# Full values kept in place in PSUM, and residual sums moved to GpSimd, in a chain of four conditioned blocks

## The chip, the cores and the metric

One core of a Trainium2 chip runs the whole program. The metric is device microseconds of that core, from one launch; the text below calls them us. The core has TensorE (PE: its matmuls; PEld: its weight loads), VectorE (DVE), ScalarE (ACT), GpSimd (POOL) and the queue of SyncE (SP), which only issues DMAs. GpSimd doesn't read or write PSUM in this kernel.

## The reference, cut to what matters

An input x of 16 batches, 256 rows of 256 float32 each, goes through four blocks. Each block has two parts, and each part is "normalise, modulate, transform, gate, add to x":

```python
norm = _ln(x) * (1.0 + scale[:, None]) + shift[:, None]      # scale, shift, gate: from a small vector per batch
h = gelu(norm @ w1 + b1)                                      # or an attention in its place
x = x + gate[:, None] * (h @ w2 + b2)
```

The eight parts are the stages 0 to 7 of the kernel. Stages 0, 1, 3, 4, 5 and 7 are two-layer networks with hidden widths of 256, 512, 1024, 512, 512 and 1024. Stage 2 is an attention with 16 heads of 64, stage 6 one with a single head of 256. In stage 4 the sum is kept only where a mask of rows says so (`where(m, fwd + bwd, 0)`), and the other rows of x stay as they are. In stage 7 a second gelu stands between h @ w2 + b2 and the gate.

## The kernel before, in words

**Numbers in two pieces.** Every matmul of values is made of three (`split3`, lines 255 to 257): a float32 value is kept as a rounded "hi" piece and a "lo" piece, lo being the full value minus hi. So each operand costs three steps outside TensorE: an activation that writes the full value, an activation that writes hi (both on ScalarE, from the same PSUM bank), and a subtraction on VectorE that writes lo. In the networks the full hidden value goes to an SBUF buffer `hf` (line 571), and VectorE subtracts `hf - hh` into `hl` (line 577). In the normalisation the full value goes to `nf` (line 392) and the subtraction is line 399.

**Stages and groups.** A network stage works on groups of two batches (512 columns), 8 groups a stage. The hidden layer is cut into chunks of 128: 2, 4, 8, 4, 4 and 8 chunks in stages 0, 1, 3, 4, 5 and 7. `ff_body` writes one group's program for each engine. For chunk c, TensorE first computes the hidden chunk c+2 (`ff_hidden`; it belongs to the next group when c+2 runs over), then the output of chunk c (`ff_output`). Two PSUM banks (`U_BANKS`) take the hidden chunks in turn, and two pairs of banks (`Y_BANKS`) take the outputs of even and odd groups.

**Order on each engine.** Each engine runs its own list in order, and semaphores tie the lists together. VectorE's list in a group of stage 1, 3, 4, 5 or 7: at c = 0 take the previous group's output (`ff_take`, line 608: output times gate into `upd`, two batches), the lo of unit 0 (`ln_rest`, line 399), the lo of a hidden chunk; at c = 1 the lo of unit 1, the statistics of the group after next (`ln_stats`, lines 320 to 330), the lo of a chunk; at c = 2 the lo of a chunk, the normalisation `xn` (`ln_norm`, line 342), the rounding of the next stage's weights (`weights_hi`, line 293), and the residual sum x = upd + xb of the previous group's first batch (`ff_add`, line 641); at c = 3 the lo of a chunk and the second batch's sum. In stage 4 the sum is a series: copy x, copy the mask's words, add, two predicated copies, copy back (lines 626 to 639). In stage 7 it is line 618.
GpSimd's list in a group: 1/sqrt (`ln_rsqrt`, line 334, one small power instruction for each of the two units), the lo of the next stage's weights (`weights_lo`, line 300), then xb = x + gated bias for this group's two batches (line 802), which waits until x of the group before is new. In stage 7 the third step is the gating after the second gelu (`ff_gate2`, line 652).
SyncE loads weight slices (when `weights_lo` of the last slice is done) and the gate rows of each batch, and in stage 7 stores x.

**Attention.** In stage 2 TensorE goes through 16 heads a batch. GpSimd divides the probabilities (line 1023), VectorE does the residual once a batch (`res_vector`, lines 1096 and 1101). Stage 6 has one turn a batch (`sh_turn`): VectorE's list is statistics of batch b+3, scaling of the probabilities, residual of b-1, lo pieces, `ln_norm` of b+3, the row maxima, the lo of the unit b+2 and the weights. One buffer `agate` holds the gate of a batch, and its load waits until the batch before has been added.

**PSUM banks of the transposes.** `ln_transpose` (line 379) writes a unit into bank 7 or 6 (in stage 0 always bank 7, in stage 2 bank 1), and the next unit for a bank waits for `ln_nf`, ScalarE's last read. Between stages that aren't chained (1 to 2, 2 to 3, 5 to 6, 6 to 7) all engines meet at a barrier (`end_phase`).

Of the kernel before, what the change touches and what calls it, by code (L numbers as in the profile page):

```python
# [31 lines left out]
GB = 2  # L32
# [11 lines left out]
def bass_cond_blocks(nc, t, out):  # L44
# [62 lines left out]
    with ctx:  # L107
# [14 lines left out]
        mcur = sb("mcur", [P, GB, TPB], I32)  # L122

        stats = [sb(f"stats{j}", [P, TPB, 6]) for j in range(GB)]
        meanvar = [sb(f"meanvar{j}", [P, TPB, 2]) for j in range(GB)]
        vareps = [sb(f"vareps{j}", [P, TPB]) for j in range(GB)]
        rstd = [sb(f"rstd{j}", [P, TPB]) for j in range(GB)]
        mhalf = sb("mhalf", [P, TPB])
        xn = [sb(f"xn{j}", [P, ROWW]) for j in range(GB)]
        nf = [sb(f"nf{j}", [P, ROWW]) for j in range(GB)]  # L130
# [14 lines left out]
        hf = [sb(f"hf{i}", [P, GW], scope=ffn) for i in range(HRING)]  # L145
# [19 lines left out]
        agate = sb("agate", [P, 2 * D], scope=att)  # L165
# [69 lines left out]
        aupd_ready = sem("aupd_ready"); ax_new = sem("ax_new"); agate_loaded = sem("agate_loaded")  # L235
# [74 lines left out]
        def ln_stats(dve, p, b, j):  # L310
            u = p * BATCH + b
            if p and early(b, 2 * GB + 2):
# [5 lines left out]
                dve.memset(spacer[:, 1:2], 0.0)  # L318
# [17 lines left out]
        def ln_norm(dve, p, b, j):  # L336
            u = p * BATCH + b
            dve.wait_ge(ln_rstd, u + 1)
            if not early(u, sets(p, b)):
                dve.wait_ge(ln_tp, u + 1 - sets(p, b))  # L340
            for k in range(TPB):
                last = dve.tensor_scalar(xn[j][:, k * D:(k + 1) * D], x[:, bass.ds(b * ROWW + k * D, D)],  # L342
                                         meanvar[j][:, k, 0:1], rstd[j][:, k:k + 1], ALU.subtract, ALU.mult)
            last.then_inc(ln_xn, 1)

        def head_norms(name, eng, p):

            for n in heads(p):
                if name == "gpsimd":
                    ln_rsqrt(eng, *n)  # L350
                else:
                    ln_stats(eng, *n)
# [1261 lines left out]
```

## Time and profile before

| what | value |
|---|---|
| median of 3 runs | 1899.54 us (1896.93 to 1900.22) |
| the profiled execution's own time | 1899.73 us |
| its span, first to last instruction | 1897.6 us |
| busy: PE | 1754.8 us, 92% of the span |
| busy: VectorE | 1355.4 us, 71% |
| busy: ScalarE | 1146.9 us, 60% |
| busy: GpSimd | 873.6 us, 46% |
| mean granted TensorE clock | 0.966 |

The stages follow each other in the trace: stage 0 up to about 130 us, stage 1 to 250, stage 2 to 1121, stage 3 to 1330, stage 4 to 1455, stage 5 to 1537, stage 6 to 1697, stage 7 to the end. A busy share is an average over stages with different limits, so the table says little by itself: what a change is worth in a stage is read from that stage's own windows and waits.

### The profile page before, as it was taken

To read this page: it belongs to the slowest core of one execution; us is meant where nothing else is said; L and a number is where in the kernel's file an instruction comes from. 1 tells how busy PE (TensorE), PEld (TensorE's weight loads), DVE (VectorE), ACT (ScalarE), POOL (GpSimd) and SP (SyncE) were. 2 spreads that over 40 slices of the span, in tenths; PEclk is the share of its full clock that TensorE was granted. 3 is DMA by queue.
4 is the path that set the end of the run, shared out by engine and by line. 5 is a ranking of instruction groups with operands and counts; after the bars stand their busy time and mean duration, and the time that the engine had idled before them with its cause. 6 is when DMAs were issued, how large, how long until landed. Compare 5 with 4: busy or idle time off the path is not lost.

```text
span 1897.6 us, 36653 instructions
## 1 busy us (share of the span) xinstructions
PE 1754.8 (92%) x12739; PEld 1587.3 (84%) x12739; DVE 1355.4 (71%) x3357; ACT 1146.9 (60%) x2858; POOL 873.6 (46%) x949
## 2 busy tenths in 40 slices
PE   5888979999999999999999979999888989989998
PEld 3657878888889888888889979999777978879997
DVE  5878866676777767677677665555999969985663
ACT  3445646666666666666666655556655746656664
POOL 1535645655665555656565533332444523331111
PEclk7999989999999999999999989999999989989999
DMA  8222200000000000000000001110111112220111
GB/s 288 64 56 70 87 20 4 10 10 10 10 10 10 9 8 10 4 10 10 10 10 10 7 15 31 29 30 27 47 43 50 52 25 44 46 58 23 45 45 45
DMA packets 110969, 65.87 MB, mean 35 GB/s; under 512 B 81530, under 2 KB 92788, under 8 KB 110788
## 3 DMA queue, kind: packets, MB, share of 16 engines
q1 hardware_dynamic: 110788, 63.54, 12.3%
q8 instruction: 104, 1.70, 0.4%
q14 instruction: 77, 0.63, 0.1%
HBM read 59.06 MB, written 4.46 MB: 33 GB/s over the span
## 4 chain that ended last, share of the span: by engine, by line
PE 77%; DVE 10%; issue 6%; ACT 5%; POOL 1%; DMA 1%; DVEq 0%; POOLq 0%; SPq 0%; ACTq 0%
PE bank L255 21%; PE bank L257 20%; PE bank L256 20%; PE bank L1036 7%; PE bank L985 6%; PE bank L379 2%; DVE xn L342 2%; DVE hl L577 1%; PE bank L438 1%; ACT nf L392 1%; DVE nTlo L399 1%; DVE aTlo L399 1%; ACT nThi L392 1%; ACT prob L1008 1%; DVE upd L608 1%
## 5 line engine op out<-in xcount | busy, mean ns | idle before, releaser
L1023 POOL TENSOR_SCALAR prob<-prob,rinv 128x256 f32<-128x256 f32 x512 | 467.3, 925 | 343.0 <-DVE rinv L1017 342.1
L571 ACT ACTIVATE hf<-bank,vecs 128x512 f32<-128x512 f32 x240 | 168.0, 700 | 302.4 <-PE bank L257 302.4
L577 DVE TENSOR_TENSOR hl<-hf,hh 128x512 fp32r<-128x512 f32 x240 | 196.7, 820 | 157.4 <-ACT hh L571 157.0
L1045 ACT ACTIVATE pthi<-bank 128x512 fp32r<-128x512 f32 x272 | 164.6, 605 | 196.5 <-PE bank L1036 193.9
L1008 ACT ACTIVATE prob<-bank,nmax 128x256 f32<-128x256 f32 x544 | 253.8, 479 | 39.6 <-DVE nmax L1281 21.1
L998 DVE TENSOR_REDUCE nmax<-bank 128x2 f32<-128x512 f32 x256 | 175.6, 686 | 142.1 <-PE bank L985 141.8
L334 POOL TENSOR_TENSOR rstd<-vareps,mhalf 128x2 f32<-128x2 f32 x128 | 106.1, 829 | 343.9 <-DVE vareps L330 343.2
L257 PE MATMUL bank<-WBhi,hh 128*128 128x256 f32 x768 | 217.7, 284 | 0.0
L256 PE MATMUL bank<-WBlo,hh 128*128 128x256 f32 x768 | 217.6, 283 | 0.0
L255 PE MATMUL bank<-WBhi,hl 128*128 128x256 f32 x768 | 217.3, 283 | 0.0
L255 PE MATMUL bank<-aThi,WAlo 128*128 128x256 f32 x576 | 177.4, 308 | 41.1 <-DVE aTlo L399 31.7
L1049 DVE TENSOR_TENSOR ptlo<-bank,pthi 128x512 fp32r<-128x512 f32 x272 | 186.2, 684 | 4.5 <-ACT pthi L1045 4.5
L255 PE MATMUL bank<-nThi,WBlo 128*128 128x512 f32 x384 | 158.0, 411 | 24.5 <-DVE nTlo L399 14.1
L392 ACT ACTIVATE nf<-bank,mod 128x256 f32<-128x256 f32 x256 | 148.1, 579 | 49.2 <-issue 28.3
L1036 PE MATMUL bank<-ident,prob 128*128 128x128 f32 x1088 | 172.6, 281 | 2.2 <-DVE prob L1291 2.0
L571 ACT ACTIVATE hh<-bank,vecs 128x512 fp32r<-128x512 f32 x240 | 167.3, 697 | 0.0
L257 PE MATMUL bank<-aThi,WAhi 128*128 128x256 f32 x576 | 166.1, 288 | 0.0
L256 PE MATMUL bank<-aTlo,WAhi 128*128 128x256 f32 x576 | 165.7, 288 | 0.0
L255 PE MATMUL bank<-pthi,vlo 128*128 128x256 f32 x512 | 148.8, 291 | 7.4 <-DVE oTlo L1078 7.4
L255 PEld LDWEIGHTS bank<-WBhi,hl 128*128 128x128 f32 x768 | 147.3, 192 | 8.1
L256 PE MATMUL bank<-nTlo,WBhi 128*128 128x512 f32 x384 | 153.6, 400 | 0.0
L256 PEld LDWEIGHTS bank<-WBlo,hh 128*128 128x128 f32 x768 | 147.1, 192 | 7.6
(164 smaller groups left out, 5310.6 us busy)
## 6 DMA issues: line engine op xcount, KB each, us to landing
gates<-gate_scratch SPq DMA_DIRECT2D x96, 256.0 KB, 3.7
agate<-gate_scratch SPq DMA_DIRECT2D x32, 256.0 KB, 3.2
stage<-in_L_cond_W SPq DMA_DIRECT2D x64, 64.0 KB, 2.3
out<-x SPq DMA_DIRECT2D x16, 256.0 KB, 2.2
adaw<-in_L_cond_Wc SPq DMA_DIRECT2D x1, 3072.0 KB, 17.9
stage<-in_L_cond_W_qkv SPq DMA_DIRECT2D x8, 384.0 KB, 3.5
x<-in_x SPq DMA_DIRECT2D x1, 2560.0 KB, 16.8
stage<-in_L_cond_ff_w SPq DMA_DIRECT2D x32, 64.0 KB, 2.1
```

Of the source, the lines that this page charges most:

```text
L255: pe.matmul(dst, lhs[1], rhs[0], start=start, stop=False, skip_group_check=True)
L256: pe.matmul(dst, lhs[0], rhs[1], start=False, stop=False, skip_group_check=True)
L257: return pe.matmul(dst, lhs[0], rhs[0], start=False, stop=stop, skip_group_check=True)
L392: last = act.activation(dst, T[:, c * SEQ:(c + 1) * SEQ], ACT.Identity, scale=mod[:, p, 0, c, bass.ds(b, 1)], bias=mod[:, p, 1, c, bass.ds ...
L571: last = act.activation(dst[:, :], U_BANKS[c % 2][:, :], ACTF[p], bias=vecs[:, at:at + 1])
L577: dve.tensor_tensor(hl[r][:, :], hf[r][:, :], hh[r][:, :].bitcast(F32), ALU.subtract).then_inc(h_lo, 1)
L998: dve.tensor_reduce(nmax[i][:, :], src.rearrange("p (q k) -> p q k", q=TPB), AX_X, ALU.max, negate=True).then_inc(nmax_ready, 1)
L1008: last = act.activation(dst[:, q, :], src[:, q * SEQ:(q + 1) * SEQ], ACT.Exp, scale=scale, bias=nmax[i][:, q:q + 1], accum_out=rsum[i][:, ...
L1023: last = pool.tensor_scalar(dst[:, q, :], dst[:, q, :], rinv[i][:, q:q + 1], None, ALU.mult)
L1036: last = pe.transpose(PTB[i][:, c * SEQ + q * P:c * SEQ + (q + 1) * P], src[:, q, c * P:(c + 1) * P], ident[:, :])
L1045: act.activation(pt[i][0][:, :], PTB[i][:, :], ACT.Copy).then_inc(pt_hi, 1)
L1049: dve.tensor_tensor(pt[i][1][:, :], PTB[i][:, :], pt[i][0][:, :].bitcast(F32), ALU.subtract).then_inc(pt_lo, 1)
```

## The change

Five edits, made together.

1. **Full values in place.** ScalarE writes hi first and then the full value over its own input in the PSUM bank. `hf` and `nf` are gone; the subtractions of lines 577 and 399 read the bank. The bank stays taken until the subtraction is done, so there are 4 U banks in place of 2 (TensorE waits for `h_lo` of four chunks back), and one pair of Y banks in place of two (the first output chunk of a group waits, bank by bank, for `y_taken` of the group before). The transposes wait for `ln_lo` in place of `ln_nf`.
2. **Residual sums on GpSimd.** `ff_add` and the new `res_add` run there. In stage 4 GpSimd adds into `act2`, and VectorE is left with two predicated copies a batch, straight into x (`ff_where`). In a group of GpSimd's list the previous group's sums (in stage 7 with the gating ahead of them) now stand first, before 1/sqrt.
3. **1/sqrt.** The addition of eps moves from VectorE to GpSimd, and the two units of a group share one addition and one power instruction.
4. **Stage 6.** `ln_norm` runs on GpSimd. Two gate buffers in place of one.
5. One-element memsets on VectorE are dropped.

```diff
@@ ln_stats, ln_rsqrt @@
-            dve.wait_ge(ln_mv, u + 1)
-            dve.tensor_scalar(vareps[j][:, :], meanvar[j][:, :, 1], EPS[p], None, ALU.add).then_inc(ln_ve, 1)
-        def ln_rsqrt(pool, p, b, j):
-            pool.wait_ge(ln_ve, p * BATCH + b + 1)
-            pool.tensor_tensor(rstd[j][:, :], vareps[j][:, :], mhalf[:, :], ALU.pow).then_inc(ln_rstd, 1)
+        def ln_rsqrt(pool, p, b, j, n=1):
+            u = p * BATCH + b
+            pool.wait_ge(ln_mv, u + n)
+            pool.tensor_scalar(vareps[:, j:j + n, :], meanvar[:, j:j + n, :, 1], EPS[p], None, ALU.add).then_inc(ln_ve, n)
+            pool.wait_ge(ln_ve, u + n)
+            pool.tensor_tensor(rstd[:, j:j + n, :], vareps[:, j:j + n, :], mhalf[:, j:j + n, :], ALU.pow).then_inc(ln_rstd, n)
+        def pool_norms(pool, units):
+            if units:
+                ln_rsqrt(pool, *units[0], len(units))
@@ ln_transpose, ln_modulate, ln_rest @@
-                pe.wait_ge(ln_nf, u if p == 0 or p == 1 and early(b, 2 * GB + 1) else u + 1 - sets(p, b))
+                pe.wait_ge(ln_lo, u if p == 0 or p == 1 and early(b, 2 * GB + 1) else u + 1 - sets(p, b))
-                for dst in (nf[j][:, c * SEQ:(c + 1) * SEQ], hi[c]):
+                for dst in (hi[c], T[:, c * SEQ:(c + 1) * SEQ]):
-            dve.tensor_tensor(lo, nf[j][:, :].rearrange("p (c r) -> p c r", c=DC), hi.bitcast(F32),
+            dve.tensor_tensor(lo, t_bank(p, b, j)[:, :].rearrange("p (c r) -> p c r", c=DC), hi.bitcast(F32),
@@ the networks @@
-        U_BANKS, Y_BANKS = bank[0:2], [bank[2:4], bank[4:6]]
+        U_BANKS, Y_BANKS = bank[0:HRING], bank[4:6]
-            if not early(n, 2):
-                pe.wait_ge(h_act, n - 1)
+            if not early(n, HRING):
+                pe.wait_ge(h_lo, n + 1 - HRING)
-            for dst in (hf[r], hh[r]):
-                last = act.activation(dst[:, :], U_BANKS[c % 2][:, :], ACTF[p], bias=vecs[:, at:at + 1])
+            for dst in (hh[r], U_BANKS[r]):
+                last = act.activation(dst[:, :], U_BANKS[r][:, :], ACTF[p], bias=vecs[:, at:at + 1])
-            dve.tensor_tensor(hl[r][:, :], hf[r][:, :], hh[r][:, :].bitcast(F32), ALU.subtract).then_inc(h_lo, 1)
+            dve.tensor_tensor(hl[r][:, :], U_BANKS[r][:, :], hh[r][:, :].bitcast(F32), ALU.subtract).then_inc(h_lo, 1)
-            if c == 0 and not early(GROUP_BASE[p] + g, 2):
-                pe.wait_ge(y_taken, GB * (GROUP_BASE[p] + g - 1))
+                if c == 0 and r % TPB == 0 and not early(GROUP_BASE[p] + g, 1):
+                    pe.wait_ge(y_taken, GB * (GROUP_BASE[p] + g - 1) + r // TPB + 1)
+        def ff_where(dve, p, g, batches=range(GB)):
+            for j in batches:
+                b = GB * g + j
+                dve.wait_ge(x_tmp, b + 1)
+                for k in range(TPB):
+                    last = dve.copy_predicated(x[:, b * ROWW + k * D:b * ROWW + (k + 1) * D],
+                                               maski[:, b * TPB + k:b * TPB + k + 1].to_broadcast([P, D]),
+                                               act2[:, j, k * D:(k + 1) * D])
+                last.then_inc(x_new, 1)
@@ ff_body, gpsimd @@
-                    for n in norms:
-                        ln_rsqrt(eng, *n)
+                    if prev and p == L3_FF:
+                        ff_gate2(eng, p, g - 1, 1 - i)
+                    if prev:
+                        ff_add(eng, *prev[:2])
+                    pool_norms(eng, norms)
...
+                    if left == 0 and not goes_on:
+                        ff_add(eng, p, g)
@@ the attentions @@
-            dve.wait_ge(axb_ready, n + 1)
-            dve.tensor_tensor(xs(b), aupd[:, :], axb[:, :], ALU.add).then_inc(ax_new, 1)
+        def res_add(pool, b, n):
+            pool.wait_ge(axb_ready, n + 1)
+            pool.wait_ge(ay_taken, n + 1)
+            pool.tensor_tensor(xs(b), aupd[:, :], axb[:, :], ALU.add).then_inc(ax_new, 1)
@@ mh_gpsimd: in the slot of head 4 @@
+                if i == 4 and not first:
+                    res_add(pool, b - 1, b - 1)
@@ sh_turn, gpsimd @@
                     ln_rsqrt(eng, *sh_batch(b + 3), n)
+                    ln_norm(eng, *sh_batch(b + 3), n)
+                if not first:
+                    res_add(eng, b - 1, BATCH + b - 1)
                 res_gpsimd(eng, b, BATCH + b)
```

## Rows read from the trace of the kernel before

**Rows 1.** Windows by stage: length, busy PE, PEld, DVE, ACT, POOL (us), clock, DMA, GB/s

```profile
130.00:250.00 120.00, 106.44 (x660) 95.56 (x660) 104.01 (x223) 67.40 (x124) 71.61 (x49) 0.95 0.27 76
...
255.00:1100.00 845.00, 808.70 (x6739) 751.65 (x6738) 587.58 (x1358) 548.08 (x1705) 505.36 (x570) 0.98 0.04 8
...
1332.00:1455.00 123.00, 103.92 (x640) 93.68 (x640) 117.29 (x362) 70.16 (x129) 50.19 (x49) 0.96 0.16 43
...
1465.00:1525.00 60.00, 60.00 (x395) 54.83 (x394) 51.80 (x129) 41.35 (x78) 31.37 (x34) 1.00 0.19 52
...
1555.00:1690.00 135.00, 126.46 (x996) 119.13 (x995) 128.01 (x333) 88.23 (x220) 40.85 (x57) 1.00 0.20 42
...
1700.00:1890.00 190.00, 188.75 (x1208) 171.39 (x1208) 104.62 (x224) 114.28 (x199) 31.45 (x29) 0.99 0.13 42
```

**Rows 2.** Line 608 in four stretches: count, min/median/max ns, first to last start

```profile
L608 DVE TENSOR_TENSOR upd<-bank,gates x15: 680/684/693, 1344.0 to 1450.8; 128x512 f32<-128x512 f32 x15
...
L608 DVE TENSOR_TENSOR upd<-bank,gates x12: 680/686/693, 1464.2 to 1525.4; 128x512 f32<-128x512 f32 x12
...
L608 DVE TENSOR_TENSOR upd<-bank,gates x16: 680/684/695, 143.3 to 239.6; 128x512 f32<-128x512 f32 x16
...
L608 DVE TENSOR_TENSOR upd<-bank,gates x14: 679/682/684, 1729.6 to 1870.8; 128x512 f32<-128x512 f32 x14
```

**Rows 3.** Who waited for line 399 in stage 4 (1332 to 1455 us): us, times

```profile
  PE bank L255: 17.8, 8
```

**Rows 4.** Groups of DVE in stage 4: count, busy us, mean ns, idle before

```profile
L577 DVE TENSOR_TENSOR hl<-hf,hh 128x512 fp32r<-128x512 f32 x33 | 31.3, 948 | 2.2 <-ACT hh L571 2.0
...
L633 DVE COPY_PREDICATED act<-mcur,upd 128x256 f32<-128x256 int32 x32 | 13.5, 476 | 0.7
...
L342 DVE TENSOR_SCALAR xn<-x,meanvar,rstd 128x256 f32<-128x256 f32 x32 | 11.0, 409 | 0.0
...
L629 DVE TENSOR_TENSOR upd<-upd,xb 128x512 f32<-128x512 f32 x16 | 10.9, 683 | 0.0
...
L627 DVE COPY act<-x 128x512 f32<-128x512 f32 x16 | 6.8, 423 | 0.0
```

**Rows 5.** The instructions that write xb, whole run: count, min/median/max ns

```profile
L802 POOL TENSOR_TENSOR xb<-x,gates x80: 1253/1301/1799, 51.9 to 1534.8; 128x512 f32<-128x512 f32 x80
```

**Rows 6.** Groups of POOL in stage 1 (130 to 250 us)

```profile
L802 POOL TENSOR_TENSOR xb<-x,gates 128x512 f32<-128x512 f32 x20 | 30.0, 1518 | 9.8 <-DVE x L641 9.8
...
L300 POOL TENSOR_TENSOR WAlo<-stage,WAhi 128x768 fp32r<-128x768 f32 x8 | 21.0, 2628 | 22.5 <-DVE WAhi L293 22.5
...
L334 POOL TENSOR_TENSOR rstd<-vareps,mhalf 128x2 f32<-128x2 f32 x13 | 11.7, 898 | 14.0 <-DVE vareps L330 13.7
...
L300 POOL TENSOR_TENSOR WAlo<-stage,WAhi 128x256 fp32r<-128x256 f32 x8 | 9.5, 1192 | 0.0
```

**Rows 7.** Who waited for line 399 in stage 6 (1555 to 1690 us)

```profile
  PEld bank L255: 11.3, 13
```

**Rows 8.** Timeline of DVE in one turn of stage 6: start, us

```profile
1614.58 1.71 DVE L342 TENSOR_SCALAR xn<-x,meanvar,rstd 128x256 f32<-128x256 f32 x2
```

**Rows 9.** A group of POOL in stage 6

```profile
L334 POOL TENSOR_TENSOR rstd<-vareps,mhalf 128x2 f32<-128x2 f32 x14 | 9.8, 700 | 3.8 <-DVE vareps L330 3.8
```

**Rows 10.** The page's costliest group (GpSimd in stage 2)

```profile
L1023 POOL TENSOR_SCALAR prob<-prob,rinv 128x256 f32<-128x256 f32 x512 | 467.3, 925 | 343.0 <-DVE rinv L1017 342.1
```

**Rows 11.** Who waited for line 399 in stage 2 (270 to 1098 us)

```profile
  PE bank L255: 27.7, 15
```

**Rows 12.** Timeline of ACT in one group of stage 7: start, us, idle before

```profile
1782.38 1.22 ACT L646 ACTIVATE act<-upd 128x512 f32<-128x512 f32 x2
...
1792.35 0.69 ACT L571 ACTIVATE hf<-bank,vecs 128x512 f32<-128x512 f32 x1 [1.55 <-PE bank L257]
```

**Rows 13.** Timeline of DVE at the very end

```profile
1892.27 2.34 DVE L618 TENSOR_TENSOR x<-x,act 128x512 f32<-128x512 f32 x2 [1.50 <-POOL act L652]
```

**Rows 14.** Timeline of PE at the start of stage 0

```profile
23.27 1.09 PE L379 MATMUL bank<-ident,xn 128*128 128x128 f32 x4 [2.18 <-ACT nThi L392]
```

More of the change, by code:

```diff
@@ L121, in bass_cond_blocks @@
         spacer = sb("spacer", [P, 8])
-        mcur = sb("mcur", [P, GB, TPB], I32)
         stats = [sb(f"stats{j}", [P, TPB, 6]) for j in range(GB)]
[L125 to L128, printed above, removed]
+        meanvar = sb("meanvar", [P, GB, TPB, 2])
+        vareps = sb("vareps", [P, GB, TPB])
+        rstd = sb("rstd", [P, GB, TPB])
+        mhalf = sb("mhalf", [P, GB, TPB])
         xn = [sb(f"xn{j}", [P, ROWW]) for j in range(GB)]
-        nf = [sb(f"nf{j}", [P, ROWW]) for j in range(GB)]
         pro = ExitStack()
@@ L164, in bass_cond_blocks @@
         aupd = sb("aupd", [P, ROWW], scope=att)
-        agate = sb("agate", [P, 2 * D], scope=att)
+        agate = [sb(f"agate{i}", [P, 2 * D], scope=att) for i in range(2)]
         smax = [sb(f"smax{i}", [P, TPB], scope=att) for i in range(2)]
@@ L311, in ln_stats @@
             u = p * BATCH + b
-            if p and early(b, 2 * GB + 2):
+            if p:
                 if p - 1 in HID:
@@ L344, in ln_norm @@
             last.then_inc(ln_xn, 1)
         def head_norms(name, eng, p):
-            for n in heads(p):
-                if name == "gpsimd":
-                    ln_rsqrt(eng, *n)
-                else:
-                    ln_stats(eng, *n)
+            if name == "gpsimd":
+                pool_norms(eng, heads(p))
             if name == "vector":
                 for n in heads(p):
+                    ln_stats(eng, *n)
+                for n in heads(p):
                     ln_norm(eng, *n)
+        def pool_norms(pool, units):
+            if units:
+                ln_rsqrt(pool, *units[0], len(units))
@@ L607, in ff_take, with ff_add @@
                 half = 1 if p == L3_FF else 0
-                dve.tensor_tensor(rows_of(upd[:, j, :]), rows_of(Y_BANKS[i][j][:, :]), gate_row(i, j, half),
+                dve.tensor_tensor(rows_of(upd[:, j, :]), rows_of(Y_BANKS[j][:, :]), gate_row(i, j, half),
                                   ALU.add if half else ALU.mult).then_inc(y_taken, 1)
-        def ff_add(dve, p, g, i, batches=range(GB)):
-            for j in batches:
+        def ff_add(pool, p, g):
+            for j in range(GB):
                 n = GB * (GROUP_BASE[p] + g) + j
@@ L845, in ff_norms @@
             if name == "gpsimd":
-                for n in ns:
-                    ln_rsqrt(eng, *n)
+                pool_norms(eng, ns)
         def ff_start(name, eng, p):
@@ L1224, in mh_gpsimd @@
                     head_norms("gpsimd", pool, A + 1)
+            if last:
+                res_add(pool, b, b)
         def mh_sync(sp, b, first, last):
```

93 lines of the change are left out of this document (33 added, 60 removed).

## The prediction, made before the changed kernel was run

> **What bounds the kernel now.** I read the windows by stage first. TensorE is busy 60.00 of 60 us in stage 5, 188.75 of 190 in stage 7 and 808.7 of 845 in stage 2; in stage 4 it is busy 103.9 of 123 while VectorE is busy 117.3, in stage 6 126.5 of 135 against VectorE's 128.0, in stage 1 106.4 of 120 against 104.0 [rows 1]. So two thirds of the time are TensorE's own, and an edit on the other engines can only lose there; stages 1, 4 and 6 are where VectorE's list sets the pace. The start times of the take (line 608) give periods: in stage 4 the groups follow each other in (1450.8 - 1344.0) / 7 = 15.26 us; in stage 5, with the same 4 chunks and the same matmuls, in (1525.4 - 0.6 - 1464.2) / 5 = 12.12 us, 0.6 being the step to the second batch; in stage 1, 4 chunks again, in (239.6 - 0.6 - 143.3) / 7 = 13.67 us [rows 2]. 12.12 is thus the floor of a four-chunk group. With 8 chunks, in stage 7, it is (1870.8 - 0.6 - 1729.6) / 6 = 23.43, so a chunk costs 2.83 and the eight transposes of a group 0.8. The waits agree: TensorE stands 17.8 us before line 399's lo pieces in stage 4 [rows 3].
>
> **Stage 4.** Off VectorE go, per batch, the add (0.683), the copy of x (0.423) and the copy back of the same shape (0.423): 1.53 x 16 = 24.5 us [rows 4]. What stays is the predicated copies. VectorE's busy time becomes 117.3 - 24.5 = 92.8 in 8.06 groups, 11.5 us a group, under the floor; eps, memsets and mask copies come off besides. The next thing that can be late is the single Y pair. The first output chunk of a group needs its bank taken. On VectorE the take stands behind the lo of a hidden chunk (0.68, as the add) and two predicated copies (2 x 0.48) [rows 4], about 1.6 us, then takes 0.68 itself [rows 2]: 2.3 us. TensorE has the eight transposes and one hidden chunk to do first, half of 2.83 since a chunk's columns are half hidden, half output: 0.8 + 1.4 = 2.2. The two are level; I add 0.45 a group for semaphores and order. So 12.6 in place of 15.26, and 12.2 for the first group of stage 5: 8 x 2.66 = 21 us. Bounds: 0 (another engine takes over at 15.26) to 25 (floor 12.12).
>
> Line 577 takes 0.948 on average here [rows 4], while line 608, of the same size but with a PSUM operand, takes 0.684 and never over 0.695 [rows 2]. The change makes line 577 such an instruction.
> The Trainium skill (SBUF — State Buffer, "Who interferes with whom") says that a VectorE instruction with two SBUF inputs contends with a GpSimd instruction that reads SBUF, and that one with at most one SBUF input doesn't. By that rule VectorE's load in stage 4 falls by another 33 x 0.26 = 8.7 us and GpSimd's adds run at their minimum; without it the durations of the rows before hold. The sum for stage 4 is the same either way, since both lie under the floor; stages 1 and 7 hang on it, through GpSimd.
>
> **Stage 1.** Its period should go from 13.67 to the floor, except where a weight slice's DMA holds VectorE's list in the first groups: I leave 3 us for that. 7 x (13.67 - 12.3) - 3 = 6.6; I take 7 us. GpSimd has to keep up, and it is in a loop with VectorE: sums of the last group, eps and power, (VectorE: normalise, round weights), lo of the weights, xb, and again. At the xb row's minimum of 1.25 [rows 5] sums and xb are 5.0, the weights 2.63 + 1.19, eps and power 1.0, VectorE's part 4 x 0.34 + 0.7: 11.9 us, just under 12.12. At the means of this stage (1.518 for sums and xb, two powers 1.8) it is 6.1 + 3.8 + 1.8 + 2.1 = 13.8 [rows 6]. I take the lower end, since fewer of VectorE's instructions meet GpSimd's. Bounds: +1 to -11 us.
>
> **Stage 6.** TensorE's weight loads stand 11.3 us in 13 turns before line 399, 0.87 a turn [rows 7]. Just ahead of it VectorE spends 1.71 on the two instructions of the normalisation [rows 8], which move to GpSimd, and 0.68 on an add as in [rows 4], which moves too. That is more than 0.87, so the wait should go: -11 us. On GpSimd the normalisation costs 2 x 0.925 by the weighing row, of the same shape with one operation in place of two [rows 10]; with power 0.70 [rows 9], eps 0.3, sum and axb 2 x 1.3 [rows 5], weights at most 1.2 [rows 6]: 6.7 us of a turn that is now 135 / 14 = 9.6, 14 being the powers there [rows 9]. Were the two-operation form twice as slow, 8.5, about the new turn of 8.7. The wait for the gate's DMA goes off GpSimd's list with the second buffer. At the stage's start one normalisation sits on the path: +1.4. Bounds: -12 to +3.
>
> **Stages 2, 3, 5.** In stage 2 TensorE waits 27.7 us, 15 times, behind transposes, four activations and line 399 [rows 11]. The chain keeps its links and their lengths: 0. GpSimd's new sum (1.3) stands in one slot of 16; it idles 343 us over 256 heads, 1.34 a slot [rows 10], so it is hidden; without that cover it would cost 1.3 x 15 = 20. Stages 3 and 5 are at the floor and stay.
>
> **Stage 7.** 1/sqrt now stands behind two gatings and two sums. The second gelus run from 1782.38 [rows 12]; the first is done at about 1783.1; four GpSimd instructions of 1.3 end at 1788.3; eps and power (0.3 + 1.1, the power on four elements estimated between 0.70 and 1.8) 1789.7; normalising 1.4, line 577 0.7: 1791.8. TensorE wants that lo when the hidden chunk whose activation starts at 1792.35 is done [rows 12]. Slack 0.5 us: I take 0, bound +8 (1.6 x 5 groups with the means above).
>
> **The ends.** At each barrier after a network, sums of 1.25 in place of 0.68 for the last two batches: +0.8, twice; after the attentions +0.6, twice. At the very end the sums stand behind both gatings: VectorE's pair starts at 1892.27, when the first gating is done, and ends at 1894.6 [rows 13]; GpSimd's second gating ends 1.25 later, at 1893.5, and two sums after it at 1896.0: +1.4. Together +4.2. At the start of stage 0 the transposes of a unit wait for the lo, not for the activation alone (TensorE stood 2.18 there [rows 14]): +0.7 twice, and the joined 1/sqrt +1.2 twice: +3.8; VectorE's lighter list returns about as much in the rest of the stage: 0, bounds -4 to +4.
>
> **The sum.** -21 - 7 - 11 + 1.4 + 4.2 = -33.4 us. The profiled execution's own time is 1899.7 (its span 1897.6), the median of the runs 1899.5, so the two scales agree: 1866.3; I say 1866.
>
> **What ScalarE's writes cost.** No row shows an activation that writes PSUM. From both sides: as now (0.69, or 1.22 for two in a row [rows 12]), or twice that for the half that is written in place. ScalarE idles 1.55 of a 2.8 us chunk in stage 7 [rows 12], but in stage 5 it is busy 41.4 of 60 and would be at 62 [rows 1]. I take "as now".
> The Trainium skill (ScalarE: Activation LUTs, "Step-by-step: what each stage is for") says that ScalarE writes PSUM faster than SBUF. By it stage 2's chain would shorten and the sum be a few us lower; no row here bears on it.
>
> **The rivals.**
> A, the forecast: 1866, chance 0.60, its own range 1855 to 1878.
> B, GpSimd becomes the bound: stage 1 at 13.8 (0 gained), stage 7 +8, stage 6 half gained. For it: the loop of 11.9 us is 0.2 under the floor. Against: GpSimd is busy only 71.6 of 120 in stage 1. -21 - 5.5 + 8 + 4.6 = -14: 1886. Chance 0.18.
> The Trainium skill (GPSIMD Engine Reference, "4.1 Engine selection") advises VectorE for elementwise work on tiles, GpSimd being about 2 times slower with two inputs. The trace agrees: 1.25 against 0.68.
> C, more than forecast: stage 4 at 12.12, stage 1 without its DMA wait, stage 0 gains 4, stage 2's chain shorter by 0.3 x 15: 1866 - 4 - 3 - 4 - 4 = 1851. Chance 0.10.
> D, slower: a bank-writing activation takes twice as long. ScalarE is then the bound of every four-chunk group: in stage 4 (70.2 x 1.5) / 8.06 = 13.1 us. Stage 4 gains 8 x 2.2 = 17, stage 1 gains 4, stage 5 loses 1 x 7, stage 2's chain is 0.9 longer 15 times, 13.5, stage 6 gains nothing, and ends and starts cost 9.4 (stage 0 without its return): +9, 1909. It decides from an extra of about 0.8 of an activation's time; at 0.5 the kernel is still faster. Against: line 608 reads PSUM at no extra cost. Chance 0.07.
> E, the edits don't do what they say, or gains and ends cancel: within 4 us of before. Chance 0.05.
>
> **Range and chances.** 1849 to 1889 holds A, B and most of C. What a measurement of this kernel tells from no change is about 0.2%, 3.8 us. Faster 0.88, same 0.05, slower 0.07.
>
> **What would show it.** Periods of line 608: 12.6 in stage 4 (15.26: something else binds; over 13: ScalarE, or the take), 12.3 in stage 1's later groups (13.8: B). Line 577 at 0.69 everywhere. No wait of TensorE before line 399 in stage 6, and 1.85 as before, 15 times, in stage 2. GpSimd's power on four elements near 1.1. In stage 7, TensorE's wait on line 577 none. The in-place activations at 0.69. The forecast is wrong if stage 4's period doesn't fall, or if TensorE's busy share in stages 2, 3, 5 or 7 does.

## The result, and the profile after

The changed kernel takes 1876.47 us (median, 1872.67 to 1880.09) beside 1899.88 for the kernel before on the same chip: a ratio of 0.9872, 95% interval 0.9851 to 0.9894. The forecast was 1866 with a range of 1849 to 1889. The direction and the range hold; of the 33 us forecast 23 came. The profiled execution took 1872.67 us, span 1870.9; it is the fastest of the four, so the two traces differ by 26.8 us where the medians differ by 23.4. One execution of the kernel with values through SBUF, further down, ran at a mean granted clock of 0.65 (2422.96 us, the others 1872 to 1878) and is left out of that kernel's times.

Where these microseconds came from is read from the starts of the takes (line 609 now), which mark every group. The sizes are differences of such starts in the two traces, and the changes are rounded last:

| stretch | before | after | change | forecast |
|---|---|---|---|---|
| start to the first take | 54.9 | 58.7 | +3.8 | +3.8 |
| rest of stage 0 | 78.8 | 75.1 | -3.7 | -3.8 |
| stage 1 (133.7 to 248.3; 133.8 to 249.2) | 114.6 | 115.5 | **+0.9** | **-7** |
| stage 2, with its ends | 901.6 | 902.1 | +0.5 | +1.4 |
| stage 3 | 179.9 | 178.6 | -1.3 | 0 |
| stage 4, to the second take of 5 | 134.3 | 115.3 | -19.1 | -21 |
| stage 5 | 71.1 | 73.2 | +2.0 | 0 |
| stage 6, with its ends | 194.3 | 183.3 | -11.0 | -8.2 (-11 + 1.4 + 0.8 + 0.6) |
| stage 7 | 159.8 | 160.2 | +0.3 | 0 |
| end | 8.1 | 9.0 | +0.8 | +1.4 |

The windows by stage answer to [rows 1] (length, busy PE, PEld, DVE, ACT, POOL, clock, DMA, GB/s):

```profile
130.00:250.00 120.00, 107.63 (x660) 96.44 (x660) 75.66 (x175) 66.68 (x124) 76.49 (x70) 0.93 0.27 76
1332.00:1455.00 123.00, 119.86 (x765) 106.99 (x764) 92.90 (x247) 81.14 (x150) 70.52 (x79) 0.99 0.20 53
1555.00:1690.00 135.00, 128.28 (x997) 122.56 (x996) 103.07 (x277) 94.73 (x226) 98.90 (x115) 0.99 0.23 50
```

In the window of stage 4 TensorE is busy 119.9 of 123 us where it was 103.9; the changed kernel leaves stage 4 at 1432.2, so 23 us of this window are stage 5, and from 1342.4 to 1432.2 it is 87.5 of 89.8. In stage 1 VectorE has lost 28 us of work and TensorE is busy barely longer: VectorE's sum of busy time was not what stage 1 waited for. The takes of stage 1, of stages 4 and 5, and of seven groups of stage 7 (answering to [rows 2]), and the page's row of the subtraction, line 577 before [rows 4]:

```profile
L609 DVE TENSOR_TENSOR upd<-bank,gates x16: 675/678/682, 142.8 to 237.3; 128x512 f32<-128x512 f32 x16
L609 DVE TENSOR_TENSOR upd<-bank,gates x16: 674/680/692, 1342.4 to 1432.8; 128x512 f32<-128x512 f32 x16
L609 DVE TENSOR_TENSOR upd<-bank,gates x14: 678/680/681, 1445.2 to 1519.0; 128x512 f32<-128x512 f32 x14
L609 DVE TENSOR_TENSOR upd<-bank,gates x14: 678/680/682, 1701.7 to 1843.0; 128x512 f32<-128x512 f32 x14
```

```profile
L578 DVE TENSOR_TENSOR hl<-bank,hh 128x512 fp32r<-128x512 f32 x240 | 163.7, 684 | 214.1 <-ACT bank L572 213.8
```

From one group to the next it is 12.46 us in stage 4 (15.26 before, forecast 12.6), 12.17 in the later groups of stage 1 (forecast 12.3) and in stage 5, 23.45 in stage 7. But the first two intervals of stage 1 are 19.40 and 13.89 (14.48 and 15.84 before) and the last is 12.56 (9.32). The others had not been alike before either: 14.67, 11.84, 12.65, 12.63 and 13.54, where it is now 11.96 and 12.17 four times. Here is the 19.40, VectorE above, TensorE below (start, us; in brackets the idle time ahead and what ended it):

```profile
152.92 0.55 DVE L286 TENSOR_SCALAR stage<-stage 128x768 f32<-128x768 f32 x1
...
155.13 0.69 DVE L578 TENSOR_TENSOR hl<-bank,hh 128x512 fp32r<-128x512 f32 x1 [0.86 <-ACT bank L572]
160.90 0.56 DVE L286 TENSOR_SCALAR stage<-stage 128x768 f32<-128x768 f32 x1 [5.08 <-DMA stage<-in_L_cond_W_out]
161.49 0.76 DVE L290 CAST WAhi<-stage 128x768 fp32r<-128x768 f32 x2
162.17 1.28 DVE L609 TENSOR_TENSOR upd<-bank,gates 128x512 f32<-128x512 f32 x2
```

```profile
157.12 0.39 PE L254 MATMUL bank<-nThi,WBhi 128*128 128x512 f32 x1
163.00 0.55 PE L252 MATMUL bank<-WBhi,hl 128*128 128x256 f32 x1 [5.49 <-DVE upd L609]
```

VectorE rounds slice 0 of the next weights at 152.9, the transfer of slice 1 can start only when GpSimd has made slice 0's low part (156.9), and lands at 160.9. Its rounding stands ahead of the take in VectorE's list, so the take starts at 162.2, and TensorE, which has only one pair to write to, stands 5.49 us. In the kernel before VectorE stood for the same slice, with the take behind it, and TensorE stood as long, one step further on, for a lo piece behind the take (VectorE, then TensorE):

```profile
156.55 0.56 DVE L289 TENSOR_SCALAR stage<-stage 128x768 f32<-128x768 f32 x1 [3.51 <-DMA stage<-in_L_cond_W_out]
```

```profile
162.13 0.80 PE L255 MATMUL bank<-nThi,WBlo 128*128 128x512 f32 x1 [5.63 <-DVE nTlo L399]
```

So the hold is not new. New are that TensorE stops at the take, with less done, and a wait of 1.93 us at 143.6 ahead of it. At 161.2, in the long wait, the granted clock falls to half (1.2 of 2.4 GHz) for 6.8 us (before: at 161.6, for 3.4). The windows of the two intervals show it (0.89 and 0.79 on average; the first also holds a fall of 3.4 us at 144.1), and that the loss lasts into the second:

```profile
142.80:162.20 19.40, 13.91 (x80) 12.38 (x80) 6.42 (x14) 8.74 (x17) 7.51 (x6) 0.89 0.11 28
162.20:176.10 13.90, 13.10 (x75) 12.09 (x76) 9.17 (x25) 3.92 (x7) 6.75 (x7) 0.79 0.29 77
```

Stages 4 and 5 begin with the same pattern in small: TensorE waits 1.74 us for a take at 1330.8, and 2.77 at 1433.1, where VectorE had stood 2.31 for a slice. So the interval over the change from stage 4 to 5 is 15.18 as before (15.21; TensorE then waited 2.88 us there, for a lo piece).

### The profile page after: what moved, and what is told of

It is laid out like the page before. It is cut to its first block, busy times and chain, and to the rows that moved or that the text cites. A ratio compares the mean times of both kernels' runs of the same rounds, so it can differ in the third digit from the quotient of the medians.

```text
span 1870.9 us, 36378 instructions
## 1 busy us (share of the span) xinstructions
PE 1743.8 (93%) x12739; PEld 1577.8 (84%) x12739; DVE 1175.4 (63%) x2800; ACT 1141.8 (61%) x2858; POOL 1007.7 (54%) x1141
## 3 DMA queue, kind: packets, MB, share of 16 engines
q1 hardware_dynamic: 110788, 63.54, 12.6%
## 4 chain that ended last, share of the span: by engine, by line
PE 83%; issue 5%; DVE 4%; ACT 3%; POOL 3%; DMA 1%; POOLq 0%; SPq 0%; DVEq 0%; ACTq 0%
PE bank L252 23%; PE bank L253 22%; PE bank L254 22%; PE bank L1026 7%; PE bank L975 6%; PE bank L380 3%; ACT bank L393 1%; DVE stats L316 1%; ACT nThi L393 1%; ACT prob L998 1%; PE bank L439 1%; POOL x L626 1%; DVE aTlo L400 1%; POOL rstd L331 1%; DVE xn L339 1%
## 5 line engine op out<-in xcount | busy, mean ns | idle before, releaser
L578 DVE TENSOR_TENSOR hl<-bank,hh 128x512 fp32r<-128x512 f32 x240 | 163.7, 684 | 214.1 <-ACT bank L572 213.8
L252 PE MATMUL bank<-aThi,WAlo 128*128 128x256 f32 x576 | 177.2, 308 | 34.6 <-DVE aTlo L400 27.2
L572 ACT ACTIVATE bank<-bank,vecs 128x512 f32<-128x512 f32 x240 | 159.6, 665 | 0.0
L254 PE MATMUL bank<-nThi,WBhi 128*128 128x512 f32 x384 | 152.5, 397 | 0.0
L254 PEld LDWEIGHTS bank<-WBhi,hh 128*128 128x128 f32 x768 | 148.5, 193 | 0.0
```

The costliest lines, as they stand in the source:

```text
L252: pe.matmul(dst, lhs[1], rhs[0], start=start, stop=False, skip_group_check=True)
L254: return pe.matmul(dst, lhs[0], rhs[0], start=False, stop=stop, skip_group_check=True)
L572: last = act.activation(dst[:, :], U_BANKS[r][:, :], ACTF[p], bias=vecs[:, at:at + 1])
L578: dve.tensor_tensor(hl[r][:, :], U_BANKS[r][:, :], hh[r][:, :].bitcast(F32), ALU.subtract).then_inc(h_lo, 1)
```

## The experiments

All times are medians, in us, with the ratio to the kernel before and its interval. "Changed" is the kernel after: one pair, in place, sums on GpSimd. Where the intervals of two ratios meet, the times alone do not tell the two kernels apart, and I go by their traces: that is so of each of the steps of 5 us or less below, and barely of the norm's place in stage 6.

### What took stage 1's gain: the order of weights and take, with one pair

**Early slice.** For the first bodies of chained stages (1, 4, 5):

```
  VectorE, c == 0, behind take and rest:   + weights_hi(eng, p + 1, 0)    (was: behind the norms, c == 2)
  GpSimd, behind ff_add:                   + weights_lo(eng, p + 1, 0)    (was: behind pool_norms)
```

> The changed kernel, with slice 0 of the next stage's weights rounded (VectorE) right behind the first take of stages 1, 4 and 5, and its low part taken (GpSimd) ahead of the 1/sqrt, instead of behind the norms; slice 1 stays at the end of the first group. Theory (one Y pair): in stage 1 the transfer of slice 1 landed at 160.9 us only because slice 0 was rounded at 152.9, VectorE stood 5.08 us for it with the take queued behind, and TensorE then stood 5.49 us before its next output chunk and fell to half its clock for 6.8 us. So the second interval between takes of stage 1 falls from 19.4 to about 15, the 5.49 us wait is gone, the 2.31 us that VectorE stands before the take at 1432.2 too; total 4 to 7 us less than the changed kernel, about 1871. Rival 1 (GpSimd's longer list in stage 1 is the cause): rounding earlier changes nothing of it, total within 1 us of the changed kernel. Rival 2 (the clock alone: it falls there whatever the wait): the wait goes, the interval stays above 17, total 1 to 2 us less.

1866.16, ratio 0.982 (0.9806 to 0.9835): 10.3 us under the changed kernel, more than expected. VectorE in the same place:

```profile
157.48 0.69 DVE L578 TENSOR_TENSOR hl<-bank,hh 128x512 fp32r<-128x512 f32 x1 [2.13 <-ACT bank L572]
158.09 0.55 DVE L286 TENSOR_SCALAR stage<-stage 128x768 f32<-128x768 f32 x1
...
159.35 1.28 DVE L609 TENSOR_TENSOR upd<-bank,gates 128x512 f32<-128x512 f32 x2
```

The 5.08 us are gone, the interval is 14.13 in place of 19.40, the next 11.65 in place of 13.89, with the clock at 1.00 in place of 0.79. But the interval ahead of both is now 10.47 for 9.01, with the clock at 0.79 for 1.00, so stage 1 gains 6.0 us in all:

```profile
134.70:145.20 10.50, 7.86 (x40) 6.91 (x40) 6.86 (x19) 5.95 (x12) 6.34 (x6) 0.79 0.55 158
...
159.40:171.00 11.60, 11.29 (x78) 10.12 (x76) 9.18 (x24) 7.49 (x15) 6.75 (x7) 1.00 0.37 93
```

The intervals at the starts of stages 4 and 5 fall by 1.6, 1.9 and 1.5 too (14.87, 15.18 and 12.98 to 13.25, 13.25 and 11.44); these, of which I had counted only the 2.31, are what exceeded the expectation. The spans of the two profiled executions differ by 7.8 us only, since stage 2, which the edit doesn't touch, took 2.7 more; over the traces of this case it takes 901.6 to 906.9. Rival 1 falls by the total, rival 2 by the interval.

**Early take.** With it, stage 0's last take ahead of the norms in its last body:

```
  VectorE, stage 0, last body, c == 1, behind rest:   + ff_take(eng, p, g, i)    (stage 1, first body: - ff_take(eng, *prev))
```

> The kernel with the early slice, and also the take of stage 0's last group put ahead of VectorE's norms and of the rest of the last layer norm in its last body. Theory: TensorE's 1.93 us wait at 143.6 us is gone, as VectorE takes the pair at about 140.1 instead of 142.8; the first take of stage 1 and all behind it come 1.5 to 3 us earlier than with the early slice alone, total about 1869. Rival: what TensorE gets there it loses at the next hidden chunk, whose inputs come later by the take's 1.3 us: no change.

1865.03, ratio 0.9814 (0.9798 to 0.983). The interval to that take falls from 10.47 to 7.42 and TensorE's longest wait for a take there from 2.6 to 1.65. The total is 1.1 us less, which the intervals don't tell apart: shown in the trace, unclear in the time.

**The kernel before with one pair.**

```
- U_BANKS, Y_BANKS = bank[0:2], [bank[2:4], bank[4:6]]
+ U_BANKS, Y_BANKS = bank[0:2], [bank[4:6], bank[4:6]]    (and TensorE waits for the take of the group before)
```

> The kernel before with one change: one pair of banks for the sums of the second layer instead of two (the other two banks idle), each half waited for by itself, as in the changed kernel. Nothing else: values still go through SBUF, sums on VectorE. Theory: the single pair is what took stage 1's gain away. Its second interval between takes goes from 14.5 to 18 or more, and there is a wait of TensorE on the take at the start of stages 1, 4 and 5; steady groups of stage 1 lengthen by at most 0.5 us each; stage 4, where VectorE is the bound, by 0 to 1 us each, since U's chunks can no longer run ahead. Total 8 to 20 us more than the kernel before, about 1912. Rival (the miss comes from GpSimd's order and the late 1/sqrt): within 3 us of the kernel before.

1938.63, ratio 1.0199 (1.0182 to 1.0216): 39 us slower, twice the upper end. The sign is as the theory says (stage 1's first intervals 21.21 and 17.37) but I had the place wrong in part: stage 1 loses 14 us, and stage 4, where I expected 0 to 1 a group, loses 18 up to the first take of stage 5, at 17.6 a group for 15.26. The takes of seven of its groups, and who waited:

```profile
L608 DVE TENSOR_TENSOR upd<-bank,gates x14: 679/686/692, 1362.3 to 1468.3; 128x512 f32<-128x512 f32 x14
...
  PE bank L255: 25.0, 7
```

That is 25.0 us in 7 waits for the take, where the kernel before waited for line 399 alone [rows 3]. With VectorE's list full, the second pair was worth 39 us.

### What the moved sums are worth

**Sums back on VectorE**, in their old places, the rest as changed (one pair):

```
  VectorE, 2 <= c < 4:   + ff_add(eng, *prev[:2], [c - 2])     (GpSimd: - ff_add(eng, *prev[:2]))
```

> The changed kernel with the sums of the networks' residuals back on VectorE, in the places where they stood before (those of the attention stages stay on GpSimd); in place and the banks as changed. In stage 4 VectorE is busy for 9.9 us of a 12.46 us group now, and two sums bring 1.4. Theory: the in-place values (no contention on 577, no 2 copies to keep) hold the gain by themselves: stage 4's groups stay within 0.4 us of 12.46, ends come 1.2 us earlier each, total within 4 us of the changed kernel. Rival: the moved sums hold the gain: they queue with norms and rests in VectorE's list, stage 4's groups take 13.3 or more (+7 us) and stage 1's 12.6 instead of 12.17, total 1884 or more.

1906.41, ratio 1.0033 (1.002 to 1.0047). My theory falls, the rival holds: 30 us, and the whole gain with them. The takes of six groups of stage 4 and who waited; then VectorE's list ahead of a take, here and in the changed kernel:

```profile
L609 DVE TENSOR_TENSOR upd<-bank,gates x12: 680/686/693, 1374.1 to 1446.7; 128x512 f32<-128x512 f32 x12
...
  PE bank L252: 10.3, 6
```

```profile
1384.31 0.68 DVE L624 TENSOR_TENSOR act<-upd,xb 128x512 f32<-128x512 f32 x1
1385.03 1.19 DVE L634 COPY_PREDICATED x<-maski,act 128x256 f32<-128x256 int32 x2
1386.11 0.68 DVE L578 TENSOR_TENSOR hl<-bank,hh 128x512 fp32r<-128x512 f32 x1
1386.71 0.67 DVE L624 TENSOR_TENSOR act<-upd,xb 128x512 f32<-128x512 f32 x1
1387.42 0.78 DVE L634 COPY_PREDICATED x<-maski,act 128x256 f32<-128x256 int32 x2
1388.34 1.29 DVE L609 TENSOR_TENSOR upd<-bank,gates 128x512 f32<-128x512 f32 x2
```

```profile
1402.43 0.79 DVE L634 COPY_PREDICATED x<-maski,act 128x256 f32<-128x256 int32 x2
1403.10 0.68 DVE L578 TENSOR_TENSOR hl<-bank,hh 128x512 fp32r<-128x512 f32 x1
1403.70 0.86 DVE L634 COPY_PREDICATED x<-maski,act 128x256 f32<-128x256 int32 x2
1404.69 1.29 DVE L609 TENSOR_TENSOR upd<-bank,gates 128x512 f32<-128x512 f32 x2
```

VectorE is busy 68.7 of 86.2 us there; it isn't full. But from the first of these lines to the take it is 4.03 us in place of 2.26, so its list ahead of the take is 1.8 us longer, the take that much later, and TensorE waits 1.7 us each time; a group takes 14.22 in place of 12.46. Is it VectorE's load that counts, or the late take alone? The banks tell it.

**Two pairs, two hidden banks, in place, sums on GpSimd:**

```
+ U_BANKS, Y_BANKS = bank[0:2] * 2, [bank[2:4], bank[4:6]]
  ff_hidden:   pe.wait_ge(h_lo, n - 1)      (for n + 1 - HRING)
  ff_output:   waits for the take of two groups back      (for the group before)
```

> The changed kernel with the banks as they were before: two banks for the hidden chunks, two pairs for the sums. Values stay in place (a hidden bank is free when VectorE has read it), sums stay on GpSimd. Theory: two hidden banks are enough for a steady group, since between the end of a chunk and the need for its bank TensorE has 4.3 us of other matmuls (1.44 + 1.4 + 1.44) and ScalarE and VectorE need 2.1 us (0.69 + 0.65 + 0.68); with two pairs the waits for the take go (1.93 and 5.49 us at 143.6 and 163.0, 1.74 and 2.77 at 1330.8 and 1433.1). Second interval of stage 1 14 to 15 us instead of 19.4, total 1861 to 1868. Rival: with two hidden banks TensorE is tied to VectorE's every delay by a chunk less, steady groups of stages 1 and 4 go from 12.2 and 12.5 to 13 or more, total above the changed kernel's 1876.

1871.11, ratio 0.9839 (0.9823 to 0.9855): better by 5, less than expected. By the traces stage 1 gains 4.7 us and stage 4 7.3, and stage 7 loses 5.3. The steady groups do as the theory says (12.17 in stages 1 and 4). The interval over stage 1's start is 16.11, above the 14 to 15 of the theory: the waits for the take are gone, but VectorE stands 5.56 us for the slice all the same, and TensorE with it, for the lo piece behind it, as in the kernel before:

```profile
162.12 0.80 PE L252 MATMUL bank<-nThi,WBlo 128*128 128x512 f32 x1 [4.00 <-DVE nTlo L400]
```

And five groups of stage 7 take 24.5 instead of 23.45. GpSimd, VectorE and TensorE's waits there:

```profile
1753.53 2.54 POOL L619 TENSOR_TENSOR x<-x,act 128x512 f32<-128x512 f32 x2
...
1756.42 1.04 POOL L331 TENSOR_TENSOR rstd<-vareps,mhalf 128x4 f32<-128x4 f32 x1
```

```profile
1757.49 1.38 DVE L339 TENSOR_SCALAR xn<-x,meanvar,rstd 128x256 f32<-128x256 f32 x4 [3.79 <-POOL rstd L331]
1758.79 1.28 DVE L578 TENSOR_TENSOR hl<-bank,hh 128x512 fp32r<-128x512 f32 x2
```

```profile
PE bank L252 <- DVE hl L578: 2.3, 3, 0.8
```

The changed kernel has the same stall of VectorE:

```profile
1738.38 1.38 DVE L339 TENSOR_SCALAR xn<-x,meanvar,rstd 128x256 f32<-128x256 f32 x4 [3.80 <-POOL rstd L331]
```

and TensorE doesn't wait: four hidden banks cover it.

**Two pairs and sums on VectorE**, the fourth corner:

> The changed kernel in place, but with two pairs and two hidden banks, and with the networks' sums back on VectorE: the fourth corner beside the changed kernel (one pair, sums on GpSimd, 1876), two pairs with sums on GpSimd (1871) and one pair with sums on VectorE (1906). Theory: sums on VectorE cost 30 us only because they stand ahead of the take in its list, and with one pair TensorE waits for each late take (1.83 us at every group of stage 4, 1.27 of stage 1). With two pairs a take may be late by a group's time: stage 4's groups fall from 14.2 to 12.2 to 12.5, stage 1's from 13.67 to 12.2, total 1870 to 1880. Rival: the load of VectorE itself is what counts (11.3 us busy and its waits do not fit into 12.2): stage 4's groups stay at 13.5 or more, total above 1890.

1867.12, ratio 0.982 (0.9804 to 0.9836). Stage 4's groups take 12.32, with no wait of TensorE on a take:

```profile
L609 DVE TENSOR_TENSOR upd<-bank,gates x14: 680/686/692, 1343.4 to 1417.3; 128x512 f32<-128x512 f32 x14
```

So it is the late take and not VectorE's load: with one pair the sums on VectorE cost 30 us, with two they cost nothing. Their median is even 4 us under GpSimd's; in the traces GpSimd then has its 1/sqrt ready in time (stage 7 at 23.45, and at the ends of stages 1 and 5 last intervals of 8.8 and 9.6 in place of 12.6 and 12.3).

| | sums on VectorE | sums on GpSimd |
|---|---|---|
| one pair, four hidden banks | 1906.4 | 1876.5 |
| two pairs, two hidden banks | 1867.1 | 1871.1 |

The upper right corner is the change; the lower left has the networks' sums and the pairs as the kernel before has them, and is 35 us faster than that kernel. So what gains is the rest: stage 4 is 21.7 us shorter there, with the values in place, two copies a batch fewer and less around the 1/sqrt, stage 6 11.7 and stage 1 6.1. No run takes the copies apart from the others. The moved sums of the networks are needed only because the pair was given up.

**Two pairs, the networks' values through SBUF again** (sums on GpSimd, layer norms in place):

```
- for dst in (hh[r], U_BANKS[r]):        + for dst in (hf[r], hh[r]):       (TensorE: wait_ge(h_act, n - 1))
```

> The kernel with two pairs and two hidden banks and sums on GpSimd (1871), but the networks' full values written to SBUF again and read from there by VectorE (layer norms stay in place). The hidden bank is then free when ScalarE is through. Theory: in place is worth only the contention and the bank it needs: the subtraction goes from 0.68 to 0.85 to 1.0 us where GpSimd runs beside it, 4 a group, 0.7 to 1.3 us of VectorE's time in stages 1, 4 and 5, which TensorE's 12.2 us still cover; stage 7's groups go from 24.5 back to 23.4 since hidden banks come free earlier: total 1865 to 1873. Rival: VectorE's list gets so long that stage 4's groups rise above 13: 1880 or more.

1872.01 (1872.00 to 1878.09), ratio 0.9855 (0.9833 to 0.9877): within what I expected, and not told apart from the 1871.1 in place. Stage 4 holds 12.2 and stage 7 comes back half way (24.0), but stage 1's middle groups go to 12.85 to 13.14. The networks' values in place are worth little here, where the sums are on GpSimd, and not the 20 of stage 4.

### Stage 6, and the ends

**Stage 6's norms back on VectorE:**

```
  GpSimd:   - ln_norm(eng, *sh_batch(b + 3), n)      VectorE, ahead of sh_max:   + the same
```

> The changed kernel with stage 6's norms (128 x 256, two a batch) back on VectorE in their old place; the sum stays on GpSimd and two gate buffers stay. Theory (as the prediction had it): the norms on VectorE were what kept stage 6 at 12.1 us a batch; the stage gets 8 to 11 us longer again, less the 1.4 us at its start, total about 1884. Rival: the sum and the in-place values had given the room already, VectorE is no longer the bound there: within 3 us of the changed kernel.

1882.52, ratio 0.9907 (0.9893 to 0.9922), 6 us over the changed kernel by the medians and 9.5 by the two spans. From stage 5's last take to stage 7's first it is 192.65 us in place of 183.32: 9.3 of the 11 are the norm's place. TensorE's weight loads wait again before the low pieces (now line 400), as in [rows 7]; in the changed kernel one such wait is left:

```profile
PEld bank L252 <- DVE vlo L400: 5.8, 7, 1.0
PEld bank L252 <- DVE aTlo L400: 3.9, 6, 1.0
```

```profile
PEld bank L252 <- DVE vlo L400: 0.3, 1, 0.3
```

**The ends**, with early slice and early take:

```
  VectorE, behind the last ff_take, if ends:    + ff_add(eng, p, g)      (GpSimd: - ff_add(eng, p, g))
  GpSimd, last body of stage 1:                 pool_norms ahead of ff_add(prev)
```

> The kernel with the early slice and the early take, and also: the last sums of stages 1 and 5 on VectorE, and GpSimd's 1/sqrt ahead of its sums in stage 1's last body. Theory: each end loses 0.6 us of its wait before the attention stage (3.43 and 3.92 us now), and the 2.52 us wait for the norm at 245.9 us falls by 1 to 1.7; total 2 to 3 us less than with both others, about 1867. Rival: the norms wait for VectorE's own list and for the statistics, not for GpSimd: only the 1.2 us of the sums.

1860.44, ratio 0.9787 (0.9771 to 0.9804), 4.6 under the kernel with early slice and take, 2 more than expected; the spans of the two profiled executions differ by 0.3. Stage 1's last interval is 11.00 in place of 12.71. The waits at the two barriers, which were to fall by 0.6 each, go from 3.4 and 4.6 us to 3.8 and 3.8.

**All of it with two pairs:**

> Everything that helped so far: the early slice, the early take, the ends, and two pairs with two hidden banks. Theory: where the takes no longer hold TensorE, two pairs add little to the kernel with the ends (1860.4 us): the 1.65 and 1.37 us left at 135.3 and 156.7, and what is left at the starts of stages 4 and 5; 1854 to 1859. Rival: two hidden banks cost more than the waits that are left: above 1862.

1863.97, ratio 0.9809 (0.9792 to 0.9825). The rival holds, as the traces have it: where the takes are early, a second pair gives 2.3 us in stage 1 and 2.1 in stage 4 (12.17 for 12.46), and two hidden banks lose 5.4 in stage 7 (24.5).

**Banks by stage:** four hidden banks and one pair in stage 7, two and two elsewhere.

> The kernel with the early slice, the early take, the ends, and two pairs with two hidden banks in all stages but the last, where there are four hidden banks and one pair. Theory: two hidden banks cost 1.05 us a group in five groups of stage 7 (0.77 us waits for VectorE's subtraction), and a second pair gives 0.3 us a group in stage 4 and 2 to 3 us around the starts of stages 1 and 5; each stage with what suits it gives about 5 us less than with two pairs everywhere (1864) : 1857 to 1860. Rival: what the second pair gives is within what the runs scatter: no better than one pair everywhere with the same ends (1860.4), by more than 1 us above it.

1857.41, ratio 0.9764 (0.975 to 0.9779), as expected; stage 7 is at 23.45 again.

**And the last bodies' sums on VectorE:**

```
  VectorE, 2 <= c < 4, ends:   + ff_add(eng, *prev[:2], [c - 2])
  GpSimd:   - if prev:         + if prev and not ends:
```

> The kernel with banks by stage, and in the last body of stages 1 and 5 the sums of the group before on VectorE too (between its subtractions), so that GpSimd has nothing but the 1/sqrt ahead of the attention stage's first norms. Theory: the waits for the norms at the ends (1.12 us at 233.5, 2.45 at 1499.1) fall to 0 and 0.6, as where all sums are on VectorE; total 2 to 4 us less than with banks by stage alone (1857.4): 1853 to 1856. Rival: the sums hold back VectorE's take and norms there, and what GpSimd gives TensorE waits for again: 1857 or more.

**1854.21, ratio 0.9748 (0.9734 to 0.9763)**, as expected: 22 us better than the changed kernel, 47 than the one before. The last body of stage 1 in the changed kernel, and then in this one (GpSimd first, then VectorE, in both):

```profile
239.71 2.54 POOL L626 TENSOR_TENSOR x<-upd,xb 128x512 f32<-128x512 f32 x2
...
242.53 0.71 POOL L331 TENSOR_TENSOR rstd<-vareps,mhalf 128x2 f32<-128x2 f32 x1
243.22 2.53 POOL L792 TENSOR_TENSOR xb<-x,gates 128x512 f32<-128x512 f32 x2
...
243.28 2.62 DVE L339 TENSOR_SCALAR xn<-x,meanvar,rstd 128x256 f32<-128x256 f32 x2 [0.71 <-POOL rstd L331]
```

```profile
229.38 0.71 POOL L331 TENSOR_TENSOR rstd<-vareps,mhalf 128x2 f32<-128x2 f32 x1
...
230.78 0.73 DVE L339 TENSOR_SCALAR xn<-x,meanvar,rstd 128x256 f32<-128x256 f32 x2
231.42 1.28 DVE L635 TENSOR_TENSOR x<-upd,xb 128x512 f32<-128x512 f32 x2
```

Two things are read there. The 1/sqrt no longer stands behind two sums; and the two norms take 0.73 us while GpSimd idles, 2.62 while GpSimd's xb runs. TensorE's waits for norms at the two ends were 2.5 and 2.3 us and are 0 and 0.6.

## Why the prediction was right, and where it was wrong

- **Stage 4, right, for a reason that was half of it.** Period 12.46 for 12.6. I subtracted 24.5 us from VectorE's load. The four corners show that with two pairs the 10.9 us of it that are sums (16 x 0.683) needn't go: 12.32 with them. What decides over the last 0.3 us, and over the sums, is the step that I put second, the take against TensorE's 2.2 us of other work ("the two are level"): 1.8 us later, as with the sums ahead of it, and TensorE waits all of it. The 2 us that are missing lie in the step to stage 5, where the take stood behind a slice.
- **Stage 1, wrong: the failed step is "Its period should go from 13.67 to the floor, except where a weight slice's DMA holds VectorE's list in the first groups: I leave 3 us for that".** 13.67 is a mean over seven unlike intervals. The last five of them were 13.07 on average and are 12.13 now: 4.7 us, and at the floor. The first two were 30.3 us together and are 33.3. That is 9.0 over twice 12.17, where I left 3; 6.0 of it stood there before, with TensorE's wait of 5.63 us, which the forecast doesn't name, and 3.0 came with the single pair. So the seven intervals gave 1.7 us for the 6.6, and the end took 3.2 back. I had worked out the single pair for the steady group of stage 4 alone and not carried it to the place where the take stands behind a transfer. That it is the transfer, the early slice shows: 5.3 us back in the first interval and 2.2 in the second, less 1.5 ahead of them. That the pair adds to it, the two pairs show: 4.7 us back in stage 1.
- **The ends, in the wrong place.** I counted the sums at the barriers (+0.8 each), where TensorE's waits did not grow (4.8 and 4.3 us before, 3.4 and 3.9 now), and not that the last body's 1/sqrt now stands behind sums in GpSimd's list, nor that xb and the norms then run side by side. Stage 1's last interval grew by 3.2 us, stage 5's by 1.8.
- **Stage 6, right**, and better than its net of -8.2: -11.0, of which 9.3 are shown to be the norm's place. GpSimd's two-operation norm takes 1.23 us, for the 0.925 by the weighing row that I used; the turn had room. Its other cost is at the stage's start, where TensorE waits 5.9 us for the first norm and waited 4.2 before; the forecast had +1.4 for it.
- **Stage 7, right, by the banks.** I gave the 1/sqrt 0.5 us of slack. In fact VectorE stands 3.80 us for it, and two hidden banks instead of four turn that into 1.05 us a group.
- **Stages 0, 2, 3 and the very end** came as forecast (stage 2's 15 waits sum to 27.2 us, 27.7 before [rows 11]; power on four elements 1.04). That the start came out at +3.8 to the tenth is luck: kernels with the same first stage reach its first take between 58.5 and 60.3 us.
- **Rivals.** B is out as a steady bound (12.17 in stage 1), but its form at the ends is real. D is out: an activation that writes its bank takes 0.665 us, 0.698 to SBUF. C had the mechanisms that the experiments then used (a DMA wait in stage 1, stage 4 at its floor), and 1851 is near what was reached, but only by further changes of order and banks.
- **The skill's rules.** The subtraction with one SBUF input is 0.684 everywhere, 0.948 in stage 4 before [rows 4]: the Trainium skill's rule (SBUF — State Buffer, "Who interferes with whom") that an instruction with at most one SBUF input doesn't contend with GpSimd, agrees. The advice of the Trainium skill (GPSIMD Engine Reference, "4.1 Engine selection") to keep two-input elementwise work on VectorE costs nothing with two pairs, 1867.1 against 1871.1, and costs 30 us with one pair, 1906.4 against 1876.5.

What stays open: how much of the early slice's gain is the granted clock and how much the wait; no run here has the one without the other. An estimate for the clock: from 161.2 to 168.0 in the changed kernel TensorE is busy 5.0 us at half speed, work of about 2.5 us at full speed, and the second interval shrank by 2.2. Not tried were the early slice on the kernel before, whose wait of 5.63 us it might remove as well, and stage 6's start (5.9 us). The waits at the barriers (3.8 us each in the last kernel) were tried with the ends alone, and stayed.

## What to carry to other kernels

Before a double buffer is given up, find in every stage the latest release of it, transfers and first groups included, and what stands ahead of the releasing instruction in its engine's list: with one buffer its delays reach TensorE (1.7 us in every group of stage 4), with two those did not. A second buffer is no cover for a transfer that holds the whole list, though: with two pairs too TensorE stood 5.63 and 4.00 us, for the next thing behind it. And don't take the mean of unlike groups for a period: look where the long ones are. An engine that isn't full can still be the bound by the order of its list, so price a moved instruction by what stands behind it on both engines. How the banks are split needn't be the same in all stages: here the last one wants hidden banks, the others pairs.

## What the runs showed of the hardware that I had not expected

- VectorE's norm (128 x 256, SBUF to SBUF) takes 0.41 us alone and 1.35 beside GpSimd's xb, as if it stood for a whole GpSimd instruction, while the subtraction that reads PSUM and SBUF stays at 0.66 to 0.69 in 240 of 240.
- An activation of 128 x 512 into the bank that it reads is not slower but a little faster than into SBUF. The order in the pair isn't the reason: before, with both into SBUF, it was 700 ns for the first and 697 for the second.

```profile
L572 ACT ACTIVATE hh<-bank,vecs 128x512 fp32r<-128x512 f32 x240 | 167.4, 698 | 284.6 <-PE bank L254 284.5
L572 ACT ACTIVATE bank<-bank,vecs 128x512 f32<-128x512 f32 x240 | 159.6, 665 | 0.0
```

- GpSimd's power grows by less than its size: 0.725 us on two elements a partition, 1.037 on four, so joining two saves 0.4.
